# A cross-attention and expert kernel: the 56 own keys laid down twice, their high and low values weighed in one matmul

## The reference, cut to what matters

```python
hidden = jnp.concatenate([context, latents], axis=1)
k = (hidden @ Wk.T).reshape(b, s_len, KV, HD)      # s_len = 1500 + 56
v = (hidden @ Wv.T).reshape(b, s_len, KV, HD)
scores = jnp.einsum('bkgqd,bksd->bkgqs', q, k) * scale
attn = jax.nn.softmax(scores, axis=-1)
out = jnp.einsum('bkgqs,bksd->bkgqd', attn, v)     # then @ Wo.T, residual
```

## Time and profile before

| what | value |
|---|---|
| median of three runs | 3404.62 us |
| the profiled execution's own time | 3410.28 us |
| its span in the trace | 3408.5 us |
| PE busy | 3314.8 us, 97% of the span |
| DVE / ACT / POOL busy | 2048.1 / 1645.9 / 1037.8 us |
| granted TensorE clock, mean | 0.986 |
| DMA | 284.52 MB, mean 83 GB/s |

### The profile page before, as it was taken

How to read it: one execution, slowest core, us unless ns; L and a number is a source line. 1 busy time by engine, 2 the same in 40 slices (tenths; PEclk the granted TensorE clock), 3 DMA queues, 4 the chain that set the end, 5 groups by cost and what they waited for, 6 DMA issues and landing times. The chain is left out here.

```text
span 3408.5 us, 64036 instructions
## 1 busy us (share of the span) xinstructions
PE 3314.8 (97%) x21457; PEld 3083.7 (90%) x21457; DVE 2048.1 (60%) x3003; ACT 1645.9 (48%) x3145; POOL 1037.8 (30%) x841
## 2 busy tenths in 40 slices
PE   8999999999999999999999999999999999999785
PEld 8989999999999999999999999999999999987674
DVE  5346666666666666666666666666666666675544
ACT  3225555555555555555555555555555555542231
POOL 0032222333233333333322232222233332345452
PEclk9999999999999999999999999999999999999887
DMA  6542222222222221222222222222222222217466
GB/s 229 200 138 59 58 64 64 64 64 61 63 61 55 52 60 57 63 64 63 64 64 64 64 64 58 64 58 58 64 64 64 64 60 60 64 49 209 128 198 210
DMA packets 308676, 284.52 MB, mean 83 GB/s; under 512 B 200968, under 2 KB 257792, under 8 KB 308631
## 3 DMA queue, kind: packets, MB, share of 16 engines
q1 hardware_dynamic: 302103, 265.56, 27.2%
q0 software_dynamic: 6528, 18.39, 1.6%
HBM read 208.31 MB, written 75.54 MB: 83 GB/s over the span
## 5 line engine op out<-in xcount | busy, mean ns | idle before, releaser
L819 PE MATMUL ps_proj<-wv_hi,parts 128*125 128x384 f32 x3072 | 875.7, 339 | 0.0
L764 DVE TENSOR_TENSOR probs_lo<-probs,probs_hi 125x448 fp32r<-125x448 f32 (+1 forms) x896 | 681.8, 777 | 275.8 <-ACT probs_hi L691 263.3
L806 PE MATMUL ps_proj<-parts,wk_hi 128*128 128x500 f32 x2304 | 710.9, 390 | 3.2 <-DVEq L719 3.2
L819 PEld LDWEIGHTS ps_proj<-wv_hi,parts 128*125 128x125 f32 x3072 | 560.0, 185 | 5.8
L144 POOL TENSOR_SCALAR parts<-raw 128x1000 fp32r<-128x1000 f32 (+1 forms) x198 | 238.4, 1204 | 959.8 <-PE ps_proj L819 780.5
L683 ACT ACTIVATE probs<-ps_scores 125x448 f32<-125x448 f32 (+1 forms) x896 | 463.0, 517 | 121.4 <-PE ps_scores L867 78.8
L819 PE MATMUL ps_proj<-wv_lo,parts 128*125 128x384 f32 x1536 | 518.4, 338 | 0.0
L806 PEld LDWEIGHTS ps_proj<-parts,wk_hi 128*128 128x128 f32 x2304 | 431.4, 188 | 91.4 <-DVEq L719 3.5
L691 ACT CAST probs_hi<-probs 125x448 fp32r<-125x448 f32 (+1 forms) x896 | 484.7, 541 | 28.3
L670 ACT CAST values_hi<-ps_proj 125x384 fp32r<-125x384 f32 x384 | 184.4, 480 | 645.2 <-PE ps_proj L819 645.2
L733 DVE TENSOR_TENSOR values_lo<-ps_proj,values_hi 125x384 fp32r<-125x384 f32 x384 | 214.3, 558 | 431.7 <-ACT values_hi L670 429.0
(11 more groups left out here) (198 smaller groups left out, 5722.3 us busy)
## 6 DMA issues: line engine op xcount, KB each, us to landing
raw<-in_ctx SPq DMA_DIRECT2D x192, 500.0 KB, 3.6
qk_hi<-proj_out_hi SPq DMA_DIRECT2D x60, 224.0 KB, 2.0
qk_lo<-proj_out_lo SPq DMA_DIRECT2D x60, 224.0 KB, 2.4
queries_hi<-qk_hi SPq DMA_DIRECT2D x32, 336.0 KB, 3.5
queries_lo<-qk_lo SPq DMA_DIRECT2D x32, 336.0 KB, 3.6
att_raw<-attended SPq DMA_DIRECT2D x128, 84.0 KB
probs<-att_raw SPq DMA_DIRECT2D x31, 336.0 KB, 5.6
probs<-inverse_sums SPq DMA_DIRECT2D x31, 336.0 KB, 3.2
```

Of the source, the lines that this page charges most:

```text
L764: dve.tensor_tensor(prs[1][0:R, u % PRING, 0:N], pr[0:R, u % PRING, 0:N], f(prs[0][0:R, u % PRING, 0:N]), ALU.subtract).then_inc(p_lo, 1)
L806: mm = pe.matmul(pproj[n % 2][:, 0:CS], w["wk"][a][:, j // 3, i * P:(i + 1) * P], ct[v][:, c, j // 3, :], start=(j == 0), stop=(j == 3 * K ...
L819: mm = pe.matmul(pproj[n % 2][0:VT, 0:KD], ct[a][:, t // VTC, j // 3, s], w["wv"][v][:, j // 3, :], start=(j == 0), stop=(j == 3 * KT - 1))
```

## The change

- **Keys.** The key tiles are now `S + 120` wide. The 56 own keys stand at `S` to `S + 56` as before and once more at `S + 64` to `S + 120`; the eight columns between are zero. The tail's `scores` take all 120 columns as stationary operand, so its probabilities come out twice, in rows 0 to 55 and 64 to 119; `exp`, `probs_hi` and `probs_lo` of the tail run over 120 partitions instead of 56.
- **Values.** The own tile of `values_hi` holds the high own values in rows 0 to 55 and the low own values in rows 64 to 119 (the column of ones stands only beside the first 56). `values_lo` has no own tile any more. The tail's `weigh` is two matmuls: this tile by the high and by the low probabilities. The low x low term is so computed too.
- **Loads.** The second copies come by eight more DMAs per batch (`load_again`), issued after `bring_back`. PE waits for them once per batch, ahead of the scores of unit 6 (group 0's tail). `load_v` writes the low values in four runs of 96 per row instead of one run of 384.
- **Start.** GpSimd clears the gap of both key tiles; the clearing of the low own values is gone.

The constants are `PAIR = 64`, `TAIL = PAIR + Q = 120`. The diff, with one renumbered wait for constants (L748, 6 for 5) left out:

```diff
 HALF = GQ // 2
+
+PAIR = 64
+TAIL = PAIR + Q
...
-        kt = [sb("keys_hi", [HD, KV, SL], F32R), sb("keys_lo", [HD + HALVES, KV, SL], F32R)]
+        kt = [sb("keys_hi", [HD, KV, S + TAIL], F32R), sb("keys_lo", [HD + HALVES, KV, S + TAIL], F32R)]
         vt_hi = sb("values_hi", [VT, NVT + 1, KV, HD + 1], F32R)
-        vt_lo = sb("values_lo", [VT, NVT + 1, KV, HD], F32R)
+        vt_lo = sb("values_lo", [VT, NVT, KV, HD], F32R)
...
         ctx_lo = stream["lo"]
-        qk_loaded, v_loaded = sem("qk_loaded"), sem("v_loaded")
+        qk_loaded, v_loaded, again_loaded = sem("qk_loaded"), sem("v_loaded"), sem("own_keys_loaded_again")
         cleared = sem("ident_cleared")
...
                 sp.sem_inc(att_stored, START)
+                def load_own(i, rows, s, loaded):
+                    sp.dma_start(f(kt[i][0:HD, 0:KTILES, s:s + Q]), rows[:, 0:HD].rearrange("i r q -> r i q")).then_inc(loaded, 16)
+                    for j in range(KTILES):
+                        sp.dma_start(f(kt[i][j * PIECE:(j + 1) * PIECE, KTILES, s:s + Q]), rows[j, HD:P]).then_inc(loaded, 16)
+
+                def load_again(b):
+
+                    for i in range(2):
+                        load_own(i, k_d[i][b], S + PAIR, again_loaded)
+
                 def load_qk(b):
                         rows = k_d[i][b]
-                        sp.dma_start(f(kt[i][0:HD, 0:KTILES, S:SL]),
-                                     rows[:, 0:HD].rearrange("i r q -> r i q")).then_inc(qk_loaded, 16)
-                        for j in range(KTILES):
-                            sp.dma_start(f(kt[i][j * PIECE:(j + 1) * PIECE, KTILES, S:SL]),
-                                         rows[j, HD:P]).then_inc(qk_loaded, 16)
+                        load_own(i, rows, S, qk_loaded)
                 def load_v(b):
-                    for i, dst in enumerate((vt_hi[0:Q, NVT, :, 0:HD], vt_lo[0:Q, NVT])):
+                    for i, dst in enumerate((vt_hi[0:Q, NVT, :, 0:HD], vt_hi[PAIR:TAIL, NVT, :, 0:HD])):
                         sp.dma_start(f(dst), scratch["v"][i].rearrange("(b q) (h d) -> b q h d", q=Q, d=HD)[b]).then_inc(v_loaded, 16)
...
                 load_qk(0)
-                sp.wait_ge(consts, 3)
+                sp.wait_ge(consts, 4)
                 load_v(0)
                         bring_back(b - 1)
+                    load_again(b)
                     for n in range(RAW, LOADS):
...
                 bring_back(B - 2)
+                load_again(B - 1)
...
                 projections_stored(pool, stream)
-                for n, ap in enumerate((f(vt_hi[:, NVT]), f(vt_lo[:, NVT]), mrow[:], ident[:], own[:])):
+                for n, ap in enumerate((f(vt_hi[:, NVT]), f(kt[0][:, :, SL:S + PAIR]), mrow[:], ident[:], own[:])):
                     pool.memset(ap, 0.0).then_inc(cleared, 1)
                     pool.wait_ge(cleared, n + 1)
-                for n, (ap, value) in enumerate(((kt[1][HD:HD + HALVES], -1.0), (vt_hi[:, 0:NVT, :, HD:HD + 1], 1.0),
-                                                 (vt_hi[0:Q, NVT, :, HD:HD + 1], 1.0))):
+                for n, (ap, value) in enumerate(((kt[1][HD:HD + HALVES], -1.0), (kt[1][:, :, SL:S + PAIR], 0.0),
+                                                 (vt_hi[:, 0:NVT, :, HD:HD + 1], 1.0), (vt_hi[0:Q, NVT, :, HD:HD + 1], 1.0))):
                     pool.memset(f(ap), value).then_inc(consts, 1)
                                    pattern=[[-1, HALF]], channel_multiplier=1).then_inc(consts, 1)
-                pool.wait_ge(consts, 4)
+                pool.wait_ge(consts, 5)
                 pool.affine_select(out=own[:], in_=own[:], compare_op=ALU.not_equal, fill=1.0, base=0,
...
                     j = u % UNITS
-                    R, N = (VT, 2 * GQ) if j < UNITS - 1 else (Q, GQ)
+                    R, N = (VT, 2 * GQ) if j < UNITS - 1 else (TAIL, GQ)
                     act.wait_ge(scores_done, b * NU + u + 1)
...
                     j = u % UNITS
-                    R, N = (VT, 2 * GQ) if j < UNITS - 1 else (Q, GQ)
+                    R, N = (VT, 2 * GQ) if j < UNITS - 1 else (TAIL, GQ)
                     act.wait_ge(exp_done, START + b * NU + u + 1)
...
                     j = u % UNITS
-                    R, N = (VT, 2 * GQ) if j < UNITS - 1 else (Q, GQ)
+                    R, N = (VT, 2 * GQ) if j < UNITS - 1 else (TAIL, GQ)
                     dve.wait_ge(p_hi, b * NU + u + 1)
...
                         pe.wait_ge(exp_done, START + b * NU + u - SBANKS + 1)
+                    if u == UNITS - 1:
+                        pe.wait_ge(again_loaded, b * 128 + 128)
                     tiles = (2 * j, 2 * j + 1) if j < UNITS - 1 else (NVT,)
                     for n, t in enumerate(tiles):
-                        s = slice(t * VT, min((t + 1) * VT, SL))
+                        s = slice(t * VT, t * VT + (VT if t < NVT else TAIL))
                         R = s.stop - s.start
...
                         pe.matmul(o, vt_hi[:, t, h], hi, start=(t == 0), stop=False)
-                        pe.matmul(pav[0:HD, h % 2, 0:GQ], vt_lo[:, t, h], hi, start=False, stop=False)
+                        if t < NVT:
+                            pe.matmul(pav[0:HD, h % 2, 0:GQ], vt_lo[:, t, h], hi, start=False, stop=False)
                         mm = pe.matmul(o, vt_hi[:, t, h], lo, start=False, stop=(t == NVT))
```

More of the change, by code:

```diff
@@ L746, in row_max @@
                 def row_max(b):
-                    dve.wait_ge(consts, 5)
+                    dve.wait_ge(consts, 6)
                     dve.wait_ge(max_done, START + b * PARTS + PARTS)
```

## The result

The changed kernel takes 3412.16 us (median of 8 runs, 3411.54 to 3416.08), the kernel before 3403.34 us (8 runs, 3399.16 to 3406.17). The ratio is 1.0031, 95% interval 1.002 to 1.0041: the change makes the kernel slower, by 8.8 us between the medians. The interval is clear of no change, though the step is only 0.3%. Forecast were 3395.4 us, a range of 3391 to 3400 us and 0.05 for slower.

The account below looks back on a forecast made before the run. PE was taken to bound the kernel but for one short stall per batch; 96 matmuls removed (9.9 us) less 0.6 us of tail cost gave 9.2 us off 3404.62, 3395.4 us, range 3391 to 3400 us.

Parts of the forecast that it names:

- Bound and worth of a matmul: PE sets the pace of `attend`; each removed tail weigh matmul is worth 0.103 us, 0.41 us per batch.
- The one stall: PE waits 0.15 us per batch before unit 10, whose low-probabilities subtract on VectorE ends only when GpSimd is done.
- Group 0's removed matmul: In unit 6, ahead of the stall: PE arrives 0.10 us earlier and waits 0.10 us longer, so nothing counted.
- Partitions are free there: Tail exponentials and splits over 120 partitions instead of 56 cost nothing on ScalarE, and likewise on VectorE.
- rival B: Tail time on ScalarE and VectorE grows with the rows, at unit 27: 19.8 us slower, 3424 us; chance 0.03.
- unit 27's removed matmul: Last removed matmul, directly ahead of the next batch's key projection; counted in full at 0.103 us.
- Does something else become late: Behind the stall, at units 26 and 27: margins of 0.17 and 0.39 us stay; at worst 0.6 us lost in all.
- Rival D: A single new stall of 0.15 us per batch takes back 4.8 us: 3400.2 us; chance 0.12.
- The loads: Eight DMAs for the second copies land by about 1573, needed at unit 6 at 1604.17: 31 us of cover.
- A: Group 0's matmul, ahead of unit 10's stall, counts too: all 128 matmuls, 11.9 us, 3392.7 us; chance 0.13.
- C: Second copies come late and PE waits at unit 6; 1 us late gives 3426 us; chance 0.02.

Follow-up runs that it names:

- E5: The kernel before, with GpSimd's last two splits of a batch held back until all 28 units' low parts are done: 3397.43 us, 0.998 of before.
- E2: The changed kernel, with VectorE's low part of the tail over 56 rows instead of 120: 3401.4 us, 0.9984 of before.
- E6: The changed kernel, with GpSimd's last two splits of a batch held back until all 28 units' low parts are done: 3392.08 us, 0.9965 of before.
- E9: The kernel before, with VectorE's low part over 120 rows in unit 6 alone: 3419.64 us, 1.003 of before.
- E1: The changed kernel, with a third matmul over an all-zero tile put back into each tail's weigh: 3422.58 us, 1.0044 of before.

## Why the prediction was wrong

- **Bound and worth of a matmul: right.** PE sets the pace, and the four removed distances were 0.10 to 0.11 us each, 0.41 us together.
- **The one stall and GpSimd's part in it: right as a mechanism.** E5 moves GpSimd away, and the stall is gone. Group 0's removed matmul adds to the stall and brings nothing where the order is that of before: in E2 the stall grows by 0.09 us.
- **"Partitions are free there. I count nothing, for VectorE by the same reason": the step that failed.** The instruction's own time is indeed the same (674 ns on average with 56 rows before and with 120 rows after; with GpSimd held back, 415 ns with 56 rows in E5 and 418 with 120 in E6), and rival B is out: there is no wait at unit 27. But on VectorE the row count of one subtract decided which of the two engines went next, 56 and 96 rows one way, 120 the other. E9 isolates it at 0.43 us per batch. The ScalarE rows that I took as the nearest could not show it: beside the same GpSimd splits ScalarE's instructions keep their time (its high parts of units 7 to 10 take 0.57 us in before and in E5, without GpSimd).
- **A second term was mis-sized: unit 27's removed matmul.** I counted it in full because it "stands directly ahead of the next batch's key projection". The turn grew by 0.13 us, so that matmul brought nothing. It does not make the change a loss, but because of it the change gains 0.21 us per batch and not the 0.29 forecast even where the order of the two engines stays (E2).
- **"Does something else become late": asked at the wrong place.** I looked behind the stall, at margins of 0.17 and 0.39 us. The late units were 8 and 9, ahead of it, which I had not priced. Unit 8 of before, VectorE's subtract and then PE's first weigh:

```profile
1519.21 1.23 DVE L764 TENSOR_TENSOR probs_lo<-probs,probs_hi 125x448 fp32r<-125x448 f32 x1
...
1521.36 0.27 PE L885 MATMUL ps_attended<-probs_hi,values_hi 125*97 125x224 f32 x1
```

It ended at 1520.44 and was used at 1521.36, a margin of 0.92 us. After, it ended at 1525.15 and PE had to wait for it until 1525.20. The margin is gone, because VectorE's backlog beside GpSimd is the outcome of a contest, and I treated it as pinned.
- **Rival D** (a new stall of 0.15 us, gains partly given back) named the kind and was off in size: two stalls of 0.25 us with 0.08 us behind each, against one before, 0.44 us per batch.
- **The balance per batch.** All figures are averages over the distances between batches. Gained: four matmuls, 0.41 us. Lost: 0.44 us in the stalls (0.66 at units 8 and 9, less 0.22 at unit 10), 0.06 and 0.07 in the two distances of the turn, 0.05 in unit 7's weigh, and under 0.01 in the tails, 0.62 in all. That makes 0.21 us of loss, and the period grew by 0.20 to 0.21. Why the turn is longer, and the second distance of unit 7's weigh, no run separates further than E1 does.
- **The loads: right.** No wait for the second copies; rivals A and C did not come about.

What stays open is why 120 rows turn the order and 96 do not. Unit 6's subtract starts 0.44 us behind GpSimd's in both kernels and takes 1.45 us in both. No run shows the arbitration itself.

## What to carry to other kernels

An instruction whose own time does not change can still change the order in which two engines get what they share, and so the time of its successors. Where VectorE and GpSimd both run on SBUF operands in the same stretch, treat every instruction of that stretch as touched. Look first whether the other engine's work can be moved out of the stretch: two lines that hold GpSimd back brought more than the change did, and made the change pay (3404.64 us before, 3397.43 with the hold alone, 3392.08 with both). Take margins as safe only where what stands ahead of them is not itself the outcome of such a contest.

## What the runs showed of the hardware

- Two instructions queued for VectorE's and GpSimd's common access with their recorded starts 0.20 us apart, and in the kernel before the later one went first; which one did was the same in all 32 batches of a kernel, and turned with the rows (96 or fewer against 120) of VectorE's instruction just before.
- A PE stall cost more than its length: the distance behind it was 0.18 to 0.19 us instead of 0.10.
- Matmuls over 56 rows between ones over 96 to 125 lost the overlap of their weight load on both sides, 0.36 us per occurrence. In the kernel before, the same product over 125 rows, 69 of them zeros, kept distances of 0.10 us.
- The turn of the batch loop grew by 0.13 us when each tail lost a matmul: 0.10 to 0.16 us up to the first matmul of the next batch, and 0.26 to 0.33 us from that one to the second.
